# Gates turned into lines through DRAM, one weight load moved behind the moves of x, and the FFN's flags regrouped, in a fused adaLN block on one core

## The reference, cut to what matters

```
mod = (silu(c) @ wmod).reshape(2, 6, 1, 512)   # sa, ca, ga, sb, cb, gb
ga, gb = sign * max(|gate|, 0.25)              # sign(0) is +
h = layernorm(x) * (1 + ca) + sa
x = x + ga * (h @ (att_w * block_mask).T)
h = layernorm(x) * (1 + cb) + sb
gate = (h @ Wg.T) * ag ;  up = (h @ Wu.T) * au   # 1376 inner features
x = x + gb * (((silu(gate) * up) @ Wd.T) * ad)
```

## Time and profile before

| | us |
|---|---|
| median of 3 runs | 178.13 (176.88 to 178.72) |
| profiled execution | 177.12 |
| its span | 175.3 |
| PE busy | 168.9 (96%) |
| DVE, ACT, POOL busy | 101.5, 81.8, 27.9 |
| TensorE's mean granted clock | 0.997 of full speed |

### The profile page before, as it was taken

One profiled execution on the slowest core, in us unless ns is written; L12 is line 12 of the kernel. 1 busy time (PEld: TensorE's weight loads), 2 busy tenths in 40 slices (PEclk: granted clock), 3 DMA queues, 4 the chain that ended last, 5 costly groups with the idle time before them and its releaser, 6 DMA issues.

```text
span 175.3 us, 2551 instructions
## 1 busy us (share of the span) xinstructions
PE 168.9 (96%) x897; PEld 128.6 (73%) x897; DVE 101.5 (58%) x213; ACT 81.8 (47%) x115; POOL 27.9 (16%) x32
## 2 busy tenths in 40 slices
PE   6889999999999999999999999999999999999992
PEld 6855454475568886888888888888888888888881
DVE  6868953993784999215755564427644214442574
ACT  3034003677996957656566443552435524352200
POOL 1323410860049210000000000006500000000000
PEclk9999999999999999999999999999999999999998
DMA  5999997999959401340300000001500000000014
GB/s 170 343 408 398 412 303 240 410 408 406 404 179 316 128 0 47 91 93 16 123 2 4 0 4 0 4 0 60 185 4 0 4 0 4 0 6 0 4 60 179
DMA packets 12389, 23.73 MB, mean 135 GB/s; under 512 B 2920, under 2 KB 5232, under 8 KB 11856
## 3 DMA queue, kind: packets, MB, share of 16 engines
q1 hardware_dynamic: 10864, 22.03, 34.7%
q10 hardware_dynamic: 1504, 1.39, 2.6%
HBM read 19.48 MB, written 2.10 MB: 123 GB/s over the span
## 4 chain that ended last, share of the span: by engine, by line
PE 79%; DVE 10%; DMA 4%; SPq 3%; issue 1%; ACT 0%; DVEq 0%
PE bank L925 39%; PE bank L995 19%; PE bank L887 14%; DMA xt<-in_x 4%; DVE bns L531 2%; PE bank L794 2%; PE bank L981 2%; DVE in_split L690 1%; DVE awork L681 1%; PE bank L866 1%; DVE modw L565 1%; SPq L252 1%; SPq L258 1%; DVE in_split L688 1%; DVE mv L533 1%
## 5 line engine op out<-in xcount | busy, mean ns | idle before, releaser
L925 PE MATMUL bank<-ht,whi_gu 128*128 128x512 f32 x352 | 83.6, 391 | 0.0
L925 PEld LDWEIGHTS bank<-ht,whi_gu 128*128 128x128 f32 x352 | 65.6, 188 | 13.9 <-issue 0.5
L681 DVE SCALAR_TENSOR_TENSOR awork<-bank,scal,awork 128x512 f32<-128x512 f32 x22 | 16.5, 751 | 51.4 <-PE bank L925 48.2
L995 PE MATMUL bank<-whi_dn,in_split 128*128 128x512 f32 x148 | 37.2, 391 | 0.2 <-issue 0.2
L491 ACT ACTIVATE awork<-bank,scal 128x512 f32<-128x512 f32 x22 | 15.2, 690 | 46.2 <-PE bank L925 46.2
L995 PEld LDWEIGHTS bank<-whi_dn,in_split 128*128 128x128 f32 x148 | 27.6, 188 | 6.1 <-issue 0.3
L887 PE MATMUL bank<-awork,wffn 128*128 128x512 f32 x64 | 30.8, 606 | 0.2 <-ACT wffn L417 0.2
L439 ACT ACTIVATE whi_gu<-wffn 128x1024 fp32r<-128x1024 f32 x22 | 23.3, 1058 | 6.9 <-PE bank L925 6.9
L887 PEld LDWEIGHTS bank<-awork,wffn 128*128 128x128 f32 x64 | 10.8, 190 | 10.1 <-issue 7.6
L432 ACT ACTIVATE junk<-wffn 128x1536 uint8<-128x1536 uint16 x11 | 16.2, 1477 | 2.4 <-DMA wffn<-in_w_down 2.4
L690 DVE TENSOR_TENSOR in_split<-awork,in_split 128x512 fp32r<-128x512 f32 x21 | 16.5, 786 | 0.7
(11 more groups left out here) (75 smaller groups left out, 111.1 us busy)
## 6 DMA issues: line engine op xcount, KB each, us to landing
wffn<-in_w_gu SPq DMA_DIRECT2D x10, 512.0 KB, 8.9
wffn<-in_w_down SPq DMA_DIRECT2D x10, 256.0 KB, 9.8
xt<-in_x SPq DMA_DIRECT2D x8, 256.0 KB, 6.0
modw<-in_mod_ln SPq DMA_DIRECT2D x4, 512.0 KB, 7.5
modw<-in_mod_gate SPq DMA_DIRECT2D x2, 1024.0 KB, 9.3
modw<-in_mod_ln SPq DMA_DIRECT2D x2, 1024.0 KB, 9.4
maskt<-in_att_mask SPq DMA_DIRECT2D x4, 256.0 KB, 8.0
awork<-in_att_w SPq DMA_DIRECT2D x4, 256.0 KB, 8.1
```

Source lines behind the costliest of these rows:

```text
L681: dve.scalar_tensor_tensor(inner[:, s % 2, :], bank[gu_bank(s, 1)][:, :], scal[:, c, 1:2], silu_g[:, s % 2, :], ALU.mult, ALU.mult).then_i ...
L925: return pe.matmul(bank[gu_bank(s, u)][:, :], w, h, start=(k == 0 and part == 0), stop=(k == KT - 1 and part == 1))
L995: last = pe.matmul(bank[4 + t][:, :], h, w, start=(c == 0 and part == 0), stop=(c == C - 1 and part == 1))
```

## The change

- The groups of chunks become 0 to 2, 3 to 6 and 7 to 10.
- `flag_vector(1)` moves from step 3 to step 1 and stays ahead of `ffn_inner`; `flag_vector(2)` stays at step 6. `read_flag` of both now stands behind `ffn_inner` of the same step. PE's `flag_sum(1)` falls to step 2 and waits for `inner_ok` 2. `read_flag(0)` and PE's `flag_sum(0)` stand later too.
- In layer 0, only sample 0's gate is still spread by PE, two `linear` calls earlier. DVE turns the gates of both samples into lines of 32x32 blocks (`gturn`), ACT writes them to DRAM with four small DMAs between `modulate(4)` and `modulate(5)`, waits for them behind `modulate(7)`, and reads sample 1's line back over all partitions (256 KB).
- In layer 1, the transposition on PE and the copy on ACT go; DVE turns the block, and SP writes the line with four small DMAs.
- On SP, `mod_ln2[0]` is issued behind the seven moves of x and the third `rows_done`, directly ahead of the other two loads that `rows_last` needs.
- On ACT, `copy_rows(3)` stands ahead of the checks and one check moves from ahead of `modulate(8)` to behind `round_gu(0)`.

```diff
+FLAG_VECTOR_AT = {1: 1, 6: 2}
-GROUPS = [(0, 4), (4, C - HELD), (C - HELD, C)]
+GROUPS = [(0, 3), (3, C - HELD), (C - HELD, C)]
...
+        def store_gate(eng, layer):
+            eng.wait_ge(gturn_ok, layer + 1)
+            line = gate_line[layer].rearrange("b k i -> (b k) i")
+            for g in range(GRP):
+                eng.dma_start(line[:, g * BLK:(g + 1) * BLK], gturn[BLK * g:BLK * g + NB * KT, layer, :])\
+                   .then_inc(d_line[layer], 16)
...
@@ sync
-            sp.wait_ge(rows_done, 2)
-            sp.dma_start(modw[:, 0, :, :], mod_ln2[0]).then_inc(d_ln2[0], 16)
             sp.wait_ge(xn_ok, XN_FIRST + TT)
             for n in range(BY_SYNC):
                 move_first(sp, n)
             sp.wait_ge(rows_done, 3)
+            sp.dma_start(modw[:, 0, :, :], mod_ln2[0]).then_inc(d_ln2[0], 16)
             sp.dma_start(modw[:, 1, :, :], mod_ln2[1]).then_inc(d_ln2[1], 16)
             sp.dma_start(modw[:, 2, :, :], mod_gate[1]).then_inc(d_gate[1], 16)
...
@@ scalar
             modulate(4)
-            copy_gate(1, bank[7])
+            store_gate(act, 0)
             modulate(5)
             modulate(6)
             modulate(7)
+            act.wait_ge(d_line[0], 16 * GRP)
+            act.dma_start(gates[:, 1, :], gate_line[0, 1].rearrange("k i -> (k i)").partition_broadcast(P))\
+               .then_inc(d_gate_first, 16)
+            copy_rows(3)
             check_chunk(next(check_at))
-            check_chunk(next(check_at))
-            copy_rows(3)
             check_chunk(next(check_at))
...
             round_gu(0)
+            check_chunk(next(check_at))
             check_chunk(next(check_at))
...
@@ vector
             flag_vector(0)
+            split(10)
             read_flag(0)
-            split(10)
             split(11)
...
-                for g, (first, _) in enumerate(GROUPS):
-                    if s == first - 1:
-                        flag_vector(g)
-                        read_flag(g)
+                if s in FLAG_VECTOR_AT:
+                    flag_vector(FLAG_VECTOR_AT[s])
                 ffn_inner(s)
+                if s in FLAG_VECTOR_AT:
+                    read_flag(FLAG_VECTOR_AT[s])
...
@@ tensor
-                (3, 1): [lambda: gate_first(0)],
-                (3, 2): [lambda: gate_first(1)],
+                (3, 0): [gate_first],
...
-                if s == 5:
-                    pe.wait_ge(gcol_ok, 1)
-                    pe.transpose(bank[3][0:KT * NB, 0:P],
-                                 gscr[:, 1, :, :].rearrange("p k b -> p (k b)"), ident[:, :])\
-                      .then_inc(gate_done, 1)
```

More of the change, by code:

```diff
@@ L102, in adaln_block @@
         gscr = sb("gscr", [P, 2, KT, NB])
-        grow = sb("grow", [KT * NB, P])
-        gate_line = nc.dram_tensor("gate_line", (NB, KT, P), F32, kind="Internal").ap()
+        gfin = sb("gfin", [P, 2, BLK])
+        gturn = sb("gturn", [P, 2, BLK])
+        gate_line = nc.dram_tensor("gate_line", (2, NB, KT, P), F32, kind="Internal").ap()
         condt = sb("condt", [P, KT, NB])
@@ L185, in adaln_block @@
         gate_ok = sem("gate_ok")
-        grow_ok = sem("grow_ok")
-        d_line = sem("d_line")
+        gturn_ok = sem("gturn_ok")
+        d_line = [sem(f"d_line{layer}") for layer in range(2)]
+        d_gate_first = sem("d_gate_first")
         d_gates = sem("d_gates")
@@ L308, in _ @@
                                  modw[BLK * i:BLK * (i + 1), 0, :, j * P:(j + 1) * P]).then_inc(d_blocks[j], 16)
[L309 to L312, removed]
+            store_gate(sp, 1)
+            sp.wait_ge(d_line[1], 16 * GRP)
             sp.wait_ge(msum_ok, KT)
             sp.dma_start(gates[:, NB:2 * NB, :].rearrange("p b n -> p (b n)"),
-                         gate_line.rearrange("b k i -> (b k i)").partition_broadcast(P))\
+                         gate_line[1].rearrange("b k i -> (b k i)").partition_broadcast(P))\
               .then_inc(d_gates, 16)
@@ L516, in _ @@
             dve.memset(sc[:, :, :], 0.0).then_inc(zeroed, 1)
+            dve.memset(gfin[:, :, :], 0.0).then_inc(zeroed, 1)
             dve.wait_ge(zeroed, 3)
@@ L635, in guard_gate @@
                 half_sign, gate = gscr[:, layer, :, :], gcol[:, layer, :, :]
+                by_batch = gfin[:, layer, 0:NB * KT].rearrange("p (b k) -> p k b", b=NB)
+                guarded = by_batch if layer == 0 else gate
                 dve.tensor_scalar(half_sign, g, 0.0, 0.5, ALU.is_ge, ALU.subtract)\
@@ L641, in guard_gate @@
                 dve.wait_ge(gate_a, layer + 1)
-                dve.scalar_tensor_tensor(gate, gate, GATE_MIN, half_sign, ALU.max, ALU.mult)\
+                if layer == 0:
+                    dve.wait_ge(zeroed, 4)
+                dve.scalar_tensor_tensor(guarded, gate, GATE_MIN, half_sign, ALU.max, ALU.mult)\
                    .then_inc(gate_m, 1)
+                dve.wait_ge(gate_m, layer + 1)
                 if layer == 1:
-                    dve.wait_ge(gate_m, 2)
                     dve.wait_ge(d_small, 48)
-                    by_batch = gscr[:, layer, :, :].rearrange("p k b -> p (k b)")\
-                        .rearrange("p (b k) -> p k b", b=NB)
                     dve.tensor_tensor(by_batch, gate, adc[:, :].unsqueeze(2).to_broadcast([P, KT, NB]),
                                       ALU.mult).then_inc(gcol_ok, 1)
+                    dve.wait_ge(gcol_ok, 1)
+                dve.transpose(gturn[:, layer, :], gfin[:, layer, :]).then_inc(gturn_ok, 1)
             def gate_linear(b, t):
@@ L654, in gate_linear @@
                 dve.wait_ge(att_done, n + 1)
-                dve.wait_ge(gate_ok, b + 1)
                 dve.wait_ge(xt_done, 3 * TT if b else TT)
                 if b:
+                    dve.wait_ge(d_gate_first, 16)
                     dve.wait_ge(x1_ok, TT)
+                else:
+                    dve.wait_ge(gate_ok, 1)
                 dve.scalar_tensor_tensor(xn[:, t, :], bank[4 * b + t][:, :], 2.0, gates[:, b, :],
@@ L884, in linear @@
                         pe.wait_ge(h_ok, 3 + t)
-                    else:
-                        pe.wait_ge(gate_ok, t - 1)
+                    if t == 2:
+                        pe.wait_ge(gate_ok, 1)
                 last = pe.matmul(bank[4 * b + t][:, :], h1[:, b, k, t * P:(t + 1) * P],
@@ L890, in linear @@
                     last.then_inc(att_done, 1)
[L892 to L898, removed]
             def flag_sum(g):
@@ L1050, in down_last, with gate_first @@
                     products(False)
-            def gate_first(b):
+            def gate_first():
                 pe.wait_ge(gate_m, 1)
-                gate_all(0, b, bank[6 + b])
+                for k in range(KT):
+                    last = pe.transpose(bank[6][:, k * P:(k + 1) * P],
+                                        gfin[:, 0, k:k + 1].to_broadcast([P, P]), ident[:, :])
+                last.then_inc(gate_done, 1)
             pe.wait_ge(ident_ok, 1)
@@ L1099, in _ @@
                         transposes(11)
+                    if (k, t) == (3, 1):
                         pe.wait_ge(modc_ok, SETS)
```

6 lines of the change are left out of this document (1 added, 5 removed).

## The result

| | before | after |
|---|---|---|
| median | 177.19 us (20 runs) | 178.25 us (20 runs) |
| ratio | | 1.0046, 95% interval 1.0026 to 1.0067 |
| profiled execution | 177.12 us | 178.06 us |
| its span | 175.3 us | 176.3 us |

The change costs 0.5%, about 0.8 us: inside the range, close to the sum of +0.75, and within 1%. One of the 20 executions after, 181.02 us at a mean granted clock of 0.990, is slow and left out of the ratio; the others had 0.997 to 1.000.

The account below looks back on a forecast made before the run. The prediction took PE to bound the kernel, busy 96% of the span. Its terms, -0.55 + 0.45 - 0.40 + 1.40 - 0.15 = +0.75 us, on a base of 177.7 gave 178.4 us, range 176.8 to 179.9.

Parts of the forecast that it names:

- the sum: All terms over the whole kernel: -0.55 + 0.45 - 0.40 + 1.40 - 0.15 = +0.75 us, with ends -0.2 to +1.75.
- Part 1: Layer 0, gate of sample 1: four transposes leave PE, -0.44 us; ACT's four DMA issues take about 2.5, cost 0.
- Part 2: mod_ln2[0] behind the moves: they land 1 to 1.5 us earlier, PE gains 0.55, then waits 0.45 at rows_last.
- "Cost 0" for ACT's list: ACT's checks after the moved load: six ahead of silu(0) either way, the moved one fills idle time, 0 us.
- Part 3: PE's flag wait at step 3: 0.57 us shrinks to some 0.15 for the flag sum, now at step 2; gain 0.40.
- Part 4: Flag 2 read behind ffn_inner(6): PE stands ahead of step 7's gate_up, +1.4 us, ends 0.9 and 1.95.
- the 0.5: Time assumed for PE's register load of the flag ahead of step 7, taken between 0 and 1.04 us.
- Part 5: Layer 1's gate: PE's transposition goes, -0.15 us with its beat; SP's four small writes cost 0.
- a base of 177.7: The mean of all four runs of the kernel before, in us, from which the forecast time was reckoned.
- the late flag costs little: Rival at step 7: load and branch run inside down's drain, costing 0 to 0.5; 177.0 to 177.6 us, chance 0.15.
- a slow register load makes all three flags late: Rival at PE's flag loads: from 0.75 us up, flags 0 and 1 cost too; sum +1.9, 179.6 us, chance 0.13.
- the load moved for nothing: Rival at the moves of x: they land as before, rows_last waits anyway; sum +1.1, 178.8 us, chance 0.1.

Follow-up runs that it names:

- e5_gates_alone: The kernel before with only both layers' gates by lines and sample 0's gate spread on PE two calls earlier; 177.16 us, ratio 1.0006.
- e1_read2_ahead: The changed kernel with read_flag(2) ahead of ffn_inner(6) again; 176.40 us, ratio to the kernel before 0.9964.
- e2_load_back: The changed kernel with SP's load of mod_ln2[0] ahead of the moves of x again; 177.85 us, ratio to the kernel before 1.0038.
- e8_read2_and_load_back: The changed kernel with read_flag(2) ahead of ffn_inner(6) and mod_ln2[0] ahead of the moves of x; 176.25 us, ratio to the kernel before 0.9958.
- e4_before_load_moved: The kernel before with only the load of mod_ln2[0] moved behind the moves of x; 178.82 us, ratio 1.0091.
- e10_before_load_and_copy: The kernel before with mod_ln2[0] behind the moves of x and copy_rows(3) ahead of the three checks on ACT; 178.71 us, ratio 1.0089.
- e3_before_read2_late: The kernel before with only read_flag(2) moved behind ffn_inner(6); 178.65 us, ratio 1.0076.
- e9_rows_later: The changed kernel with read_flag(2) ahead of ffn_inner(6) and rows_last one linear call later on PE; 176.05 us, ratio to the kernel before 0.9936.
- e7: The changed kernel with flag 2's register loaded twice in a row ahead of step 7; 179.97 us, ratio to the kernel before 1.0128.
- e11: The changed kernel with read_flag(2) ahead of ffn_inner(6) and flag 2's register loaded twice; 176.81 us, ratio to the kernel before 0.9974.

## Why the prediction was right, step by step

- **Part 1, the gate of sample 1.** PE's four transposes went and ACT's DMA issues cost nothing, as forecast; they took 1.6 us for four, not 2.5. Together with the wait of part 2, PE's own way to `rows_last` shrank by 0.55 us, from 9.78 to 9.23, as forecast. That the 0.44 needs an earlier landing of the moves to be worth anything is shown by e5_gates_alone.
- **Part 2, the load.** The moves landed in a median of 2.1 us in place of 4.0. DVE's turn came at 28.14 against 29.89, 1.75 us sooner, of which 0.30 is x itself; the other 1.45 is inside the forecast. The last load landed at 36.9, inside 36.0 to 37.3. PE stood 0.65 us for it, and 1.05 in e1_read2_ahead with the same code up to there, where 0.45 was taken: the term was too small. That the move is a wash is shown in the timing by e2_load_back and e8_read2_and_load_back. "Cost 0" for ACT's list held, but for a reason that the text passed over: it counted six checks either way and called the moved one a filler, when the places of that check and of the copy are what keeps the load's move from costing 1.6 us (e4_before_load_moved, e10_before_load_and_copy).
- **Part 3, the flag of step 3.** Forecast -0.40 with the flag sum at step 2 counted in; measured -0.86 + 0.12 = -0.74. The term was mis-sized: I took the visible gap from 67.02 to 67.59 alone. The entry behind it in the earlier trace rows, `down` with 2.11 us for 8 matmuls against 1.81 elsewhere, held another 0.3.
- **Part 4, the flag of step 6.** Forecast +1.4, ends 0.9 and 1.95; measured +1.65, with the cause shown from both sides by e1_read2_ahead and e3_before_read2_late. The read ended 0.48 us behind the beat, where 0.57 was forecast, and from there to the weights it was 1.17, where I took 0.34 + 0.5. The forecast says that no row shows the register load. That was wrong: the trace of the kernel before has it three times under its own line, and with it the 0.5 need not have been a guess:

```profile
L917 PEldq TENSOR_LOAD <-flags x3: 305/310/496, 47.2 to 84.6; - x3
L917 PEldq FUSED_REGOPS  x3: 146/151/160, 47.8 to 85.0; - x3
L917 PEldq SEQ_ASSERT  x3: 18/18/24, 48.0 to 85.2; - x3
```

The Trainium skill ("DMA: Bandwidth & Descriptors", Latency and other measured facts) has about 600 ns as the floor of such a load. The TENSOR_LOAD rows here are below it, 0.30 to 0.31 us for flags 1 and 2 and 0.50 for flag 0; 0.64 is what a whole `value_load` adds, register operations and check included.

- **Part 5.** Forecast -0.15, measured -0.16.
- **The sum.** The parts as measured in the two profiles are -0.55 + 0.69 - 0.74 + 1.65 - 0.16 = +0.89. With the +0.10 from ahead of them (x 0.30 sooner, 0.40 lost waiting for ACT) this is the +0.99 of the ledger, against +0.75 forecast; the timing has about +0.8. The wait for the loads and the late flag were each sized too small by about 0.25, the flag of step 3 by 0.34 the other way: the mechanisms were right, but that the sum came so close is in part luck. So is the forecast of 178.4 beside the measured 178.25: it went on a base of 177.7, and the median before is 177.19.
- **The rivals.** That the late flag costs little is refuted by e1 and e3. That a slow register load makes all three flags late was half right. At flag 1 the changed kernel has 1.20 us and just makes its beat. At flag 0 it has 1.14 us to the beat and takes 1.43, since the load is 0.50 there, so the weights of `gate_up(0)` come 0.3 late (0.53 against 0.24); PE has matmuls queued and does not wait. Where the read ends 0.70 us ahead of the beat, 0.42 us show (e9_rows_later). That the load moved for nothing is true in a sense the text didn't have: the moves did land earlier, and in the timing it still won nothing.

## What to carry to other kernels

A value that chooses a branch must be ready long before the branch: here 1.17 us (1.43 at the first flag) lie between the end of the write of the flag and the first weights, and only a stretch of work already queued on PE can hide them, so on the writing engine the flag's read goes ahead of the bulk of the same step. Before taking work off the engine that bounds, look for the next wait behind it: a PE step that was removed in front of a DMA wait was worth nothing, and when the wait was filled with other PE work (e9_rows_later) a flag that had been covered till then took back half of it. When a load is moved back, follow everything queued behind it, through the last consumer's list: here the places of a check of weights and of a copy, both on ACT, decided whether the move cost 0 or 1.6 us. And before a cost is called unknown, ask the trace for the line itself: the page leaves out register and branch instructions, the line's own view has them.

## What the runs showed of the hardware

- A load of a value into a register of PE's sequencer shows as TENSOR_LOAD with 0.30 to 0.31 us, and 0.50 the first time in the execution, in the kernel before, the changed one, e1, e3, e7, e9 and e11. With its register operations (0.15) and check (0.02) it adds 0.64 us (e7). The compare and branch behind it is 0.32 in the changed kernel at step 7. From the flag's end to the weights it is 1.17 and 1.22 us with one load (changed kernel, e3), 1.81 with two (e7, e11), and 1.43 at flag 0 (changed kernel, e9).
- The seven 64 KB moves that SP issues took a median of 4.0 to 4.5 us to land with a 1 MB load issued ahead of them (before, e2, e8), and 2.1 with it behind them (changed kernel, e1, e4, e9).
- TensorE's clock fell behind a stand of 1.90 us in full work (e7: 0.57 and 0.58 in the means of 88 to 90 and 90 to 92) and did not behind one of 1.26 us in the changed kernel's profile. The fall cost 1.5 us, more than twice the 0.64 that caused it, and four of e7's six timed executions show it by their mean clock and time. The shorter stand is not proven safe: one of 20 executions of the changed kernel had a mean clock of 0.990 and took 181.02 us; where in it the clock fell is not recorded.
- A stall can be longer than the idle time shown before it: behind the stand at step 3 of the kernel before, the next 8 matmuls took 2.11 us in the chain against 1.81 elsewhere, and only the distance between the weight loads of two steps (6.30 against 5.44) gave the whole 0.86.
